# Two code moves in the self-attention stage: the first Q projection ahead of the previous unit's second O projection, and that projection's residual behind a division

## The reference, cut to what matters

```python
x = x + xattn(layernorm(x), ctx, ctx, mask, W_Q, W_K, W_V, W_O)      # cross attention, 512 keys
x = x + attn(layernorm(x), Wq, bq, Wk, bk, Wv, bv, Wo, bo)           # self attention, 64 tokens
x = x + ffn(layernorm(x), W1, b1, W2, b2)                            # ternary weights, relu
# attn: Q, K, V = proj(x); scores = Q @ K^T / sqrt(32)
#       top-k of min(64, S) = all 64 scores; softmax; @ V; @ Wo.T + bo
```

## Time and profile before

| What | Value |
|---|---|
| median of 3 runs | 1724.17 us |
| the profiled execution's own time | 1724.65 us |
| its span, first to last instruction | 1722.8 us |
| TensorE busy | 1662.9 us (97%) |
| VectorE busy | 1068.9 us (62%) |
| ScalarE busy | 699.8 us (41%) |
| GpSimd busy | 212.0 us (12%) |
| mean granted clock of TensorE | 0.992 |

### The profile page before, as it was taken

The page is one execution under the profiler, slowest core; times in us unless marked ns, Lnnn a source line. Parts: engine busy times, 40 slices in busy tenths (PEclk is TensorE's granted clock), DMA queues, the critical chain, the costliest instruction groups (busy, mean ns, idle before and its releaser), DMA issues.

```text
span 1722.8 us, 38414 instructions
## 1 busy us (share of the span) xinstructions
PE 1662.9 (97%) x16012; PEld 1390.8 (81%) x16012; DVE 1068.9 (62%) x1492; ACT 699.8 (41%) x1657; POOL 212.0 (12%) x300
## 2 busy tenths in 40 slices
PE   6899999999999999998999999999799999999999
PEld 4688888888878888876888888888688888888887
DVE  3655565555555565676688778787785455545633
ACT  2555556655556556665523222222222222222221
POOL 1000000000000000121202121211032022202200
PEclk9999999999999999999999999999899999999999
DMA  6011111111111111344111111111321122112110
GB/s 221 13 62 62 63 63 56 57 62 63 59 45 51 59 57 63 110 174 164 41 50 61 49 61 49 61 47 51 93 57 54 45 53 72 51 28 70 39 36 25
DMA packets 83484, 111.78 MB, mean 65 GB/s; under 512 B 7840, under 2 KB 48928, under 8 KB 82080
## 3 DMA queue, kind: packets, MB, share of 16 engines
q1 hardware_dynamic: 83360, 109.95, 20.2%
HBM read 67.97 MB, written 25.17 MB: 54 GB/s over the span
## 4 chain that ended last, share of the span: by engine, by line
PE 91%; DVE 5%; issue 1%; ACT 1%; DMA 1%; SPq 0%; DVEq 0%; ACTq 0%
PE project L350 51%; PE project L1285 13%; PE scores L718 4%; PE scores L1780 3%; PE scores L1778 3%; PE probs_t_psum L1780 3%; PE probs_t_psum L1778 3%; PE probs_t_psum L727 3%; PE attended_t L744 2%; PE probs_t_psum L1394 2%; PE attended_t L1413 1%; PE scores L522 1%; DVE self_at_lo L1597 1%; DVE self_residual L1633 1%; DVE row_sum L1622 0%
## 5 line engine op out<-in xcount | busy, mean ns | idle before, releaser
L1285 PE MATMUL project<-ff_xt,w_ternary 128*128 128x512 f32 x1024 | 253.1, 389 | 0.0
L1295 ACT ACTIVATE hidden<-project,b_sb 128x512 f32<-128x512 f32 x128 | 88.2, 689 | 339.0 <-PE project L1285 336.0
L1285 PEld LDWEIGHTS project<-ff_xt,w_ternary 128*128 128x128 f32 x1024 | 192.1, 188 | 39.8
L904 ACT ACTIVATE cross_scores_probs<-cross_scores_probs,exp_bias,logit_scale 128x128 f32<-128x128 f32 x256 | 122.8, 485 | 101.6 <-DVE exp_bias L1047 101.6
L350 PE MATMUL project<-self_xt_hi,self_w_hi 128*128 128x256 f32 x512 | 149.2, 291 | 2.7 <-DVE self_xt_lo L534 1.6
L350 PE MATMUL project<-self_xt_lo,self_w_hi 128*128 128x256 f32 x512 | 145.8, 285 | 0.0
L350 PE MATMUL project<-self_xt_hi,self_w_lo 128*128 128x256 f32 x512 | 145.7, 285 | 0.0
L904 ACT ACTIVATE cross_probs<-cross_scores,exp_bias,logit_scale 128x128 f32<-128x128 f32 x256 | 122.9, 485 | 1.8 <-DVE exp_bias L1047 1.8
L350 PE MATMUL project<-ctx_hi,cross_w_hi 128*128 128x512 f32 x256 | 106.1, 414 | 14.8 <-DVE ctx_lo L1066 14.8
L350 PE MATMUL project<-cross_w_hi,ctx_hi 128*128 128x512 f32 x256 | 108.7, 425 | 0.0
L350 PEld LDWEIGHTS project<-self_xt_hi,self_w_hi 128*128 128x128 f32 x512 | 99.2, 194 | 5.7 <-issue 2.6
(11 more groups left out here) (169 smaller groups left out, 4068.0 us busy)
## 6 DMA issues: line engine op xcount, KB each, us to landing
ctx_raw<-in_ctx SPq DMA_DIRECT2D x64, 256.0 KB, 3.8
cross_xt_raw<-in_x_t SPq DMA_DIRECT2D x64, 128.0 KB, 2.1
cross_x<-in_x SPq DMA_DIRECT2D x32, 256.0 KB, 2.9
x<-cross_x SPq DMA_DIRECT2D x32, 256.0 KB, 2.0
self_x<-x SPq DMA_DIRECT2D x32, 256.0 KB, 2.8
self_x_norm<-self_blocks_t SPq DMA_DIRECT2D x64, 128.0 KB, 2.7
ff_w_raw<-in_w SPq DMA_DIRECT2D x2, 4096.0 KB, 13.9
x<-self_residual SPq DMA_DIRECT2D x32, 256.0 KB, 2.0
```

The lines of the kernel that those rows point to most:

```text
L904: last = nc.scalar.activation(c_p[buf][:, cols], c_s[buf][:, cols], ACT.Exp, bias=exp_bias[:, buf, g:g + 1], scale=logit_scale[:, parity(u ...
L1285: last = nc.tensor.matmul(PJ[m % 2][:], w1_q[:, c, cols], x_t[parity(v)][:, c].rearrange("p n a r -> p (n a r)"), start=(c == 0 and x_t is ...
L1295: nc.scalar.activation(h_raw[:, m % 2, :], PJ[m % 2][:], ACT.Relu, bias=b1_sb[:, m:m + 1]).then_inc(h_relu, 1)
```

## The change

In a unit's step, TensorE now does the Q0 projection directly behind the first scores, and the O projection of the unit before (O1) behind Q0. On VectorE the residual that reads this O projection moves from behind `maxima(u, 0)` to behind `divide(u, 0)`. This holds in units 1 to 14. No instruction of the work is added or taken away.

```diff
@@ self_pe, step
                 if not is_unit(u, 0):
                     scores(u, 0)
+                    qk_proj(u, "Q0", 0, kind)
                     o_proj(later(u, -1), 1, "full")
-                    qk_proj(u, "Q0", 0, kind)
                 qk_proj(u, "Q1", 0, kind)
                 scores(u, 1)
                 transposes(u, 0)
@@ self_dve, step
                 maxima(u, 0)
+                if kind == "full":
+                    self_ln_statistics(e, w)
+
+                    wait(e, G.stats, total(w, NT, NT))
+                divide(u, 0)
                 if not is_unit(u, 0):
                     residual(later(u, -1), 1, "full")
-                if kind == "full":
-                    self_ln_statistics(e, w)
-
-                    wait(e, G.stats, total(w, NT, NT))
-                divide(u, 0)
                 if kind == "full":
                     self_ln_aggregate(e)
                 maxima(u, 1)
```

More of the change, by code:

```diff
@@ L1663, in step @@
                 maxima(u, 0)
-                if not is_unit(u, 0):
-                    residual(later(u, -1), 1, "full")
                 if kind == "full":
@@ L1670, in step @@
                 divide(u, 0)
+                if not is_unit(u, 0):
+                    residual(later(u, -1), 1, "full")
                 if kind == "full":
```

## The result

| | kernel before | changed kernel |
|---|---|---|
| median | 1724.89 us (6 runs, 1723.85 to 1726.86) | 1772.01 us (6 runs, 1766.73 to 1773.83) |
| ratio to before | 1 | 1.0267, 95% interval 1.0251 to 1.0283 |
| span of the profiled execution | 1722.8 us | 1772.0 us |
| mean granted clock | 0.992 | 0.983 |

What follows compares the result with a forecast made beforehand. TensorE was taken as the bound, 91% of the chain of waits. Stalls of 33.5 us and clock falls of 13 us made 46.5 us, 1771.2 against the profiled 1724.65; forecast 1770 us, range 1752 to 1784.

Steps and rivals of the forecast that it cites:

- Q0 early wins 0.45 us a unit: TensorE, self stage: Q0 ahead of O1 removes O1's wait for the low attended values, 6 us in 14 units.
- Q1 waits for bank 0: TensorE, ahead of Q1: O1 has just filled bank 0, and Q1 needs the residual to empty it first.
- Both halves cost: Ahead of Q1: some 0.9 us of wait with the residual in its old place; the residual also goes behind the division.
- the cover of Q0: TensorE, between O1 and Q1: Q0 hid the wait for the residual that empties bank 0; the change takes it away.
- The chain of 4.72 us from the statistics: VectorE: load lands, statistics, row sums, reciprocal, scaling, residual, then Q1; unit 7's Q1 starts 2.4 us later.
- 33.5 us of stalls: TensorE ahead of Q1, units 1 to 14: the later starts of Q1 together, 2.4 to 2.7 us in most units.
- 8 falls at 1.6 us, 13 us: TensorE's clock behind the stalls: 8 falls in 14 units, 13 us; the ends were none and 14 at 1.75, 24.5 us.
- rival 1: The stall without the clock: granted clock stays near 1.00, only 33.5 us added, 1758 us; chance 0.14.
- The lower of the two bounds: TensorE's clock: after an idle stretch of 2.0 us before the change it stayed at 2.4 GHz, without a fall.
- Nothing behind Q1 gives this back: Rest of a unit: it follows TensorE, which had no other wait there, so Q1's delay is not recovered.
- GpSimd has slack: GpSimd: its work starts some 4.3 us later behind the late residual, with slack.
- Rival 3: Faster: residual done by O1's end, possible only with another bank; 0.41 us wait gone, 1718 us; chance 0.04.

Runs made afterwards that it cites:

- e7: Against e4, GpSimd computes the reciprocal deviation ahead of the additions that wait for the late residual's store; 1716.85 us, ratio 0.9960.
- e4: Against the changed kernel, the two PSUM banks are dealt out in TensorE's new order of use, so Q1 takes Q0's bank; 1734.93 us, ratio 1.0062.
- e1: Against the changed kernel, the residual goes back behind the first maxima, so only TensorE's order is changed; 1738.45 us, ratio 1.0081.
- e2: Against the changed kernel, TensorE keeps O1 ahead of Q0, so only the residual is moved, behind the division; 1769.27 us, ratio 1.0254.
- e6: Against the changed kernel, SP's store of tile 0 moves behind the load of the next unit's tokens; 1739.79 us, ratio 1.0093.
- e9: The changed kernel as it is, measured again for comparison on the same chip as e10; 1772.65 us, ratio 1.0273.
- e10: Against the changed kernel, eight matmuls that nobody reads between O1 and Q1 in units 1 to 14; 1761.76 us, ratio 1.0215.
- e5: Against the changed kernel, six matmuls that nobody reads between O1 and Q1 in units 1 to 14; 1766.19 us, ratio 1.0245.
- e3: Against the changed kernel, the statistics of unit u+2 and their wait for the load stand behind the residual; 1740.71 us, ratio 1.0090.

## Why the prediction was right

- **Q0 early wins 0.45 us a unit.** Right. The wait for the low part is gone in 13 units, 5.9 us. e7, where nothing takes it back, has a unit of 28.71 us against 29.24.
- **Q1 waits for bank 0.** Right, and shown by e4, where the bank alone is changed and the wait is gone.
- **Both halves cost.** Q1's wait with the residual in its old place was put at 0.9 us; e1 has 0.8. That the cover of Q0 doesn't save the late residual is shown by e2, 44 us slower by itself.
- **The chain of 4.72 us from the statistics.** 4.75 us in unit 7, and the scaling takes 1.23 us as taken. Its start at the landing of the load is right, and e6 shows that the load binds it. This was the step least visible before, since the residual ended just as the load landed.
- **33.5 us of stalls.** 33.5 us in the table of waits. In detail unit 3 has 4.60 us of idle time and not 3.5 + 0.5, unit 1 2.44 us and not 2.9, and these cancel in part; the exact agreement is luck. e9, the same kernel once more, waits 41.5 us for the residual instead of 42.7.
- **8 falls at 1.6 us, 13 us.** 8 falls in the profile, 11.7 us, and e10 shows that they cost this. That falls come was right, and it is what separates 1770 from rival 1's 1758. The number was a guess between none and 14, and that it was met is luck: e9's profile has 8 as well, in part in other units, but the six executions of the changed kernel go from 1766.73 us at a mean clock of 0.987 to 1773.83 at 0.983. The lower of the two bounds between which it was guessed, no fall at 2.0 us of idle time, is none: e5 and e10 have falls behind 1.8 to 1.9 us. Why the clock falls just in these units stays open.
- **Missing from the sum:** what the pauses cost beside their length, 1.8 us. In the stretch of the self stage 47.0 us were measured and 46.5 forecast. The profiled execution took 1773.83 us where 1771.2 was forecast for it; the larger part of that miss, 2.2 us, lies outside the stretch and isn't the change's.
- **"Nothing behind Q1 gives this back", and GpSimd has slack.** Right for the changed kernel, whose own stall gives GpSimd the time. As a statement on the late residual it is wrong: without the stall GpSimd's chain binds at once, and made e4 slower than the kernel before. I had followed the residual's store to the additions, and not to the reciprocal deviation behind them.
- **Rival 3, faster, if O1 and Q1 had different banks.** I gave it 1718 us. The banks alone gave 1735; with GpSimd's order changed too it was 1717.

## What to carry to other kernels

When a block is moved in a list that shares buffers in turn, ask which block now follows the one that fills the same buffer, and deal the buffers out anew in the new order. A drain that is moved later takes everything with it that waits for the drain, the stores, the next reuse, and whatever stands behind those on each engine's list; follow it to the end. And where a stall of two to three microseconds comes in every unit, add the clock's falls to its length.

## What was unexpected of the hardware

Idle stretches of 1.8 to 3.2 us were followed by a fall of TensorE's clock in some units and not in others, and the longer did not decide it. In the changed kernel unit 5 (2.90 us idle) fell, unit 7 (2.96 us) and unit 12 (3.14 us) did not. In e2, whose stalls in units 4 to 13 are 2.3 to 2.7 us, unit 13 fell behind 2.36 us and unit 5 did not behind 2.41 us. With the filler ahead of the idle rest, e5 fell behind 1.82 and 1.87 us, e10 behind 1.88 us. Behind e3's stalls of 1.4 us there was none. A fall cost 1.50 us (4.63 against 3.13 us for 24 matmuls), and a single pause some 0.1 us beside its length (Q1 to the second scores in 3.07 us against 2.97), even where the clock stayed up.
